# Four of the next tile's projection groups moved into the output projection's loop, and a shorter rounding sequence on VectorE

## The chip, the cores and the metric

One Trainium2 chip, all 8 of its cores, one launch. Each core works on one of the 8 sequences of the batch; no core waits for another, but they share the chip's memory. The metric is the device time in microseconds (us) of the slowest core. Engines: TensorE (PE) multiplies matrices, VectorE (DVE), ScalarE (ACT) and GpSimd (POOL) work elementwise, and DMAs are issued from instruction queues, here above all from the one of SyncE (SP).

## The reference

`x` is 8 sequences of 2048 tokens with 1024 features. The kernel computes

```
xz = x @ Win.T ; xi, z = split(xz)                 # 2 x 2048 features
lam = exp(-8 * softplus(omega) * sigmoid(xi @ Wl.T + bl))
v   = xi @ Wv.T + bv
h_t = lam_t * (h_{t-1} - 2 v_t (v_t.h_{t-1}) / (v_t.v_t)) + (1 - lam_t) * xi_t
x1  = layernorm(x + (silu(z) * h) @ Wout.T)
xq  = clip(round(x1 / scale), -127, 127) * scale    # scale: one number
out = layernorm(x1 + xq @ (ternary - 1).T + bias)
```

The change touches the order of work around `Wout` and the `round` in `xq`.

## The kernel before

A core takes its 2048 tokens in 8 tiles of 256 tokens. Every operation is recorded in program order by `Rec.do` into one list for each engine; an engine executes its own list strictly in that order, and waits on semaphores only where the recorded tokens (`waits=`) say so. DMAs recorded for "sync" stand in SP's list, so a waiting DMA holds up every DMA behind it.

The stages of a tile, in PE's order:

- **lambda and v projections** (L290 to L360, L466 to L538): bf16 matmuls, the weights (`WLV`) streamed in 1 MB steps.
- **gram, chain 0, dhg 0, chain 1, dhg 1**: the recurrence, solved in two chunks of 128 tokens. `chain` alternates small PE and ACT steps; `dhg` runs on VectorE and GpSimd and ends in `LAMb`, the bf16 high and low parts of silu(z)*h.
- **output projection** (L836 to L896): for both halves `dg` of the 1024 output features and 16 slices `ic`, 2 x 3 bf16 matmuls of 128x512. In tile 0 the weights come as f32, 256 KB for each `ic` (`w_out`), VectorE splits them (L853, L858) and two stores write the parts to `wos`; SP's order is load, two stores (which wait for the split), next load. In the other tiles two slices (a *pair*) are loaded at once from `wos`, 2 x 256 KB, into one of two buffers; a load waits until the matmuls of the pair two earlier are done (`wou_free`).
- **layer norm, rounding, transposes, FFN**, for each chunk `tc` of 128 tokens: VectorE adds the residual (L941), `ln` normalises, then eight VectorE instructions on 128x1024 f32 round (L947 to L965). PE transposes the result (L972) as soon as the last of them, L965, is done, and multiplies with the ternary weights (`WFF`). VectorE goes to chunk 1 only after chunk 0's L965.

Into these stages the *first* projection of the **next** tile (`x @ Win.T`) is woven, in 32 *groups* (`emit_s1_group`): a 512 KB load of weights on SP into one of two `WIN` slots (free when the group two earlier is done), eight f32 matmuls (16 records in the trace) into bank `ec % 3`, and an eviction. Groups 0 to 15 give `xi`, 16 to 31 `z`. `pump(n)` emits up to n groups at that place in all lists: 7 ahead of chain 0, one for each of its 7 steps, 2 in chain 1, then 8 at L823 (groups 16 to 23), 2 and 1 before the two chunks' transposes, and 5 at the tile's end. A z group's eviction (L266) overwrites `ZS`, so it waits for `zgate`, the end of dhg 1. With three banks, PE can run groups 16, 17 and 18 while dhg 1 works; group 19 waits for L266. In the last tile there is no next tile, and `pump` does nothing.

Of the kernel before, what the change touches and what calls it, by code (L numbers as in the profile page):

```python
# [8 lines left out]
AL = mybir.AluOpType  # L9
# [36 lines left out]
def build(n_tiles=8):  # L46
    T = n_tiles * TT
    nc = bass.Bass("TRN2", target_bir_lowering=False)
    r = Rec()
# [82 lines left out]
    FFS = sb("FFS", [128, D], F32)  # L132
# [39 lines left out]
    for k in range(NDC):  # L172
# [3 lines left out]
                  waits=(t_cv,))  # L176
        t_cv = r.do("vector", lambda e, a=stg[:, sl * 1024:(sl + 1) * 1024],
                    o=WFF[:, k * D:(k + 1) * D]:
                    e.tensor_scalar_add(o, a, -1.0),
                    waits=(t_l,), inc="dv")  # L180
    t_wffn = t_cv
    t1 = r.do("scalar", lambda e: e.activation(WOM2[:, :], WOM[:, :], AF.Exp),
              waits=(t_pro,), inc="ac")
    t1 = r.do("scalar", lambda e: e.activation(WOM2[:, :], WOM2[:, :], AF.Ln, bias=1.0),
              waits=(t1,), inc="ac")
    t_wom = r.do("vector", lambda e: e.tensor_scalar_mul(WOM2[:, :], WOM2[:, :], -8.0),
                 waits=(t1,), inc="dv")
    t_wom = r.do("vector", lambda e: e.tensor_scalar_mul(WOMN[:, :], WOM2[:, :], -1.0),
                 waits=(t_wom,), inc="dv")
    t_zro = r.do("vector", lambda e: e.memset(ZRO[:, :], 0.0), inc="dv")  # L190
    t_s1 = r.do("vector", lambda e: e.tensor_scalar_max(A1[0:1, 0:1], A1[0:1, 0:1], 1e-5),
                waits=(t_sc,), inc="dv")
    t_s2 = mm(pb[4][:, 0:1], CON[0:1, 0:128], A1[0:1, 0:1], True, True,
              waits=(t_s1, t_con), inc="pe")
    t_s3 = r.do("vector", lambda e: e.tensor_copy(SB_[:, :], pb[4][:, 0:1]),
                waits=(t_s2,), inc="dv")
    drain[4] = t_s3
    t_rs = r.do("vector", lambda e: e.reciprocal(RSC[:, :], SB_[:, :]),
                waits=(t_s3,), inc="dv")
# [74 lines left out]
    for tile in range(n_tiles):  # L274
# [9 lines left out]
        for tc in range(TT // 128):  # L284
            t_xtm = dma("gpsimd", XTM[:, xto + tc * D:xto + (tc + 1) * D],
                        d_xtm[t0 + tc * 128:t0 + (tc + 1) * 128, :], "dxt",
                        waits=(xtm_free[0],))
        t_lam = [None] * NIC
        t_sig = [None] * NIC
        for jc in range(NIC):  # L290
            sl = jc % 2
            if tile == 0:
# [4 lines left out]
                else:  # L297
# [3 lines left out]
                          waits=(tjsp[p],))  # L301
# [3 lines left out]
                            waits=(t_l, tjmm2[p], tjout2[p], tjsp[p]),  # L305
                            inc=jsem)
# [3 lines left out]
                               waits=(t_js,), inc=jsem)  # L310
                dma("sync", d_wls[jc][:, 0:N], wslotb[:, 0:N], "dgl%d" % p,
                    waits=(tjsp[p],))
# [4 lines left out]
            else:  # L317
# [3 lines left out]
                          waits=(wlv_free[sl],) + split_done["wl"])  # L321
                t_w2 = dma("sync", wslotb[:, N:2 * N], d_wls[jc][:, N:2 * N],
                           "dl%d" % (sl + 2),
                           waits=(wlv_free[sl],) + split_done["wl"])
# [11 lines left out]
            for ic in range(NIC):  # L336
# [3 lines left out]
                   waits=(t_xi[NIC - 1],) if ic == 0 else ())  # L340
            for ic in range(NIC):
# [4 lines left out]
                         waits=(t_w2,) if ic == 0 else (),  # L346
                         inc="pe" if ic == NIC - 1 else None)
# [4 lines left out]
            if jc % 2 == 1:  # L352
                for j2 in (jc - 1, jc):
                    tev = r.do("scalar", lambda e, o=fm(KK, j2, 0, TT),
                               i=pb[bank][:, (j2 % 2) * TT:(j2 % 2) * TT + TT],
                               b=BLc[:, j2:j2 + 1]:
                               e.activation(o, i, AF.Sigmoid, bias=b),  # L357
                               waits=(tok,) + tuple(t_hprev), inc="ac")
# [3 lines left out]
        for jc in range(NIC):  # L362
            t_lam[jc] = r.do("scalar", lambda e, o=fm(LAM, jc, 0, TT),
                             i=fm(KK, jc, 0, TT), s=WOM2[:, jc:jc + 1]:
                             e.activation(o, i, AF.Exp, scale=s),  # L365
                             waits=(t_wom, t_sig[jc], t_gprev), inc="ac")
        for jc in range(NIC):
# [3 lines left out]
                              waits=(t_lam[jc],), inc="ac")  # L371
# [43 lines left out]
        if tile != 0:  # L415
            t_rb = r.do("vector", lambda e: e.reduce_sum(
                SB0[:, :].unsqueeze(2), fm3(LAM, 0, L), X),
                waits=(t_bh, t_state_pe), inc="dv")
            t_rb = r.do("vector", lambda e: e.tensor_add(
                SB0[:, :], SB0[:, :], STATE[:, :]),  # L420
                waits=(t_rb, t_state), inc="dv")
# [44 lines left out]
        for jc in range(NIC):  # L466
            sl = jc % 2
            if tile == 0:
# [4 lines left out]
                else:  # L473
# [3 lines left out]
                          waits=(tjsp[p],))  # L477
# [3 lines left out]
                            waits=(t_l, tjmm2[p], tjout2[p], tjsp[p]),  # L481
                            inc=jsem)
# [3 lines left out]
                               waits=(t_js,), inc=jsem)  # L486
                dma("sync", d_wvs[jc][:, 0:N], wslotb[:, 0:N], "dgv%d" % p,
                    waits=(tjsp[p],))
# [4 lines left out]
            else:  # L493
# [3 lines left out]
                          waits=(wlv_free[sl],) + split_done["wv"])  # L497
                t_w2 = dma("sync", wslotb[:, N:2 * N], d_wvs[jc][:, N:2 * N],
                           "dl%d" % (sl + 2),
                           waits=(wlv_free[sl],) + split_done["wv"])  # L500
# [11 lines left out]
            for ic in range(NIC):  # L512
# [3 lines left out]
                   waits=(t_xi[NIC - 1],) if ic == 0 else ())  # L516
# [34 lines left out]
        if tile == 0:  # L551
# [7 lines left out]
            for ic in range(NIC):  # L559
# [8 lines left out]
                       waits=(tok,), inc="dv")  # L568
# [32 lines left out]
        def pump(n=1):  # L601
            for _ in range(n):
                if s1n is None or s1n["ec"] >= 2 * NIC:
                    return
                if s1n["ec"] >= NIC and s1n["zgate"] is None:
                    return
                emit_s1_group(s1n)
# [212 lines left out]
        t_gfull = t_g21  # L820
        if s1n is not None:
            s1n["zgate"] = list(t_g21)
        pump(8)  # L823
        t_state = r.do("vector", lambda e, i=fm3(GC, TT - 1, TT).squeeze(2):
                       e.tensor_copy(STATE[:, :], i),
                       waits=(t_state_pe,) + tuple(t_h), inc="dv")
# [9 lines left out]
        for dg in range(2):  # L836
            for ic in range(NIC):
                sl = (ic // 2) % 2
                if tile == 0:
                    p = ic % 2  # L840
                    if p == 0:
                        slotf = WOU[:, 0:512]
                        wslotb = WOU.bitcast(BF16)[:, 2048:3072]
                    else:
                        slotf = Y1[:, 0:512]
                        wslotb = Y1.bitcast(BF16)[:, 2048:3072]
                    jeng, jsem = "vector", "dv"
                    kw = (tjout2[1], tjsp[1]) if wofirst[1] and p == 1 else ()
                    wofirst[p] = False
                    t_l = dma("sync", slotf, d_wo[dg, ic], "wo%d" % p,  # L850
                              waits=(wosp[p],) + kw)
                    t_js = r.do(jeng, lambda e, o=wslotb[:, 0:512], i=slotf:
                                e.tensor_copy(o, i),  # L853
                                waits=(t_l, womm[p], woout[p], wosp[p]) + kw,
                                inc=jsem)
                    wosp[p] = r.do(jeng, lambda e, o=wslotb[:, 512:1024],
                                   i=slotf, h=wslotb[:, 0:512]:
                                   e.tensor_tensor(o, i, h, AL.subtract),  # L858
                                   waits=(t_js,), inc=jsem)
                    dma("sync",  # L860
                        d_wos[dg, ic // 2][:, (ic % 2) * 1024:(ic % 2) * 1024 + 512],
                        wslotb[:, 0:512], "dgo%d" % p, waits=(wosp[p],))
                    woout[p] = dma("sync",
                                   d_wos[dg, ic // 2][:, (ic % 2) * 1024 + 512:
                                                      (ic % 2) * 1024 + 1024],
                                   wslotb[:, 512:1024], "dgo%d" % p, waits=())
                    t_w = wosp[p]
                    split_done["wo"] = (woout[0], woout[1], wosp[0], wosp[1])
                else:
                    slotb = WOU.bitcast(BF16)[:, sl * 2048:(sl + 1) * 2048]  # L870
                    if ic % 2 == 0:
                        t_wo2 = dma("sync", slotb[:, 0:1024],
                                    d_wos[dg, ic // 2][:, 0:1024],
                                    "wo%d" % sl,
                                    waits=(wou_free[sl],) + split_done["wo"])
                        t_wo2b = dma("sync", slotb[:, 1024:2048],
                                     d_wos[dg, ic // 2][:, 1024:2048],
                                     "wo%d" % (sl + 2), waits=())
                    t_w = t_wo2 if ic % 2 == 0 else t_wo2b
                    wslotb = slotb[:, (ic % 2) * 1024:(ic % 2 + 1) * 1024]  # L880
                for tc in range(TT // 128):
                    bank = 4 + 2 * dg + tc
                    gh = LAMb[:, ic * 2 * TT + tc * 256: ic * 2 * TT + tc * 256 + 128]
                    gl = LAMb[:, ic * 2 * TT + tc * 256 + 128:
                              ic * 2 * TT + tc * 256 + 256]
                    w0 = ((t_w, drain.get(bank)) + tuple(t_g2c[tc])) \
                        if ic == 0 else (t_w,)
                    mm(pb[bank][:, 0:512], gh, wslotb[:, 0:512],
                       ic == 0, False, waits=w0)
                    mm(pb[bank][:, 0:512], gl, wslotb[:, 0:512], False, False)  # L890
                    gtok[2 * dg + tc] = mm(pb[bank][:, 0:512], gh,
                                           wslotb[:, 512:1024],
                                           False, ic == NIC - 1, inc="pe")
                wou_free[sl] = gtok[2 * dg + (TT // 128) - 1]
                t_jmm = wou_free[sl]
                womm[ic % 2] = t_jmm  # L896

        if tile == 0:
            split_done["stage"] = split_done["stage"] + (wosp[1], woout[1])
# [29 lines left out]
        for tc in range(TT // 128):  # L929
# [3 lines left out]
            for dg in range(2):  # L933
# [13 lines left out]
            tq = r.do("vector", lambda e, o=r1s, i=y1s: e.tensor_scalar(  # L947
                o, i, RSC[:, :], 127.0, AL.mult, AL.min),
                waits=(t_y1[tc], t_rs, txq), inc="dv")
            tq = r.do("vector", lambda e, o=r1s: e.tensor_scalar_max(o, o, -127.0),  # L950
                      waits=(tq,), inc="dv")
            tq = r.do("vector", lambda e, o=FFSI[:, :], i=r1s: e.tensor_copy(o, i),
                      waits=(tq,) + split_done["stage"], inc="dv")
            tq = r.do("vector", lambda e, o=scr, i=FFSI[:, :]: e.tensor_copy(o, i),
                      waits=(tq,), inc="dv")
            tq = r.do("vector", lambda e, o=FFS[:, :], i=r1s, k=scr:
                      e.scalar_tensor_tensor(o, i, -0.5, k, AL.add, AL.is_ge),
                      waits=(tq,), inc="dv")
            tq = r.do("vector", lambda e, o=r1s, k=scr:
                      e.scalar_tensor_tensor(o, o, 0.5, k, AL.add, AL.is_le),  # L960
                      waits=(tq,), inc="dv")
            tq = r.do("vector", lambda e, o=FFS[:, :], i=r1s:
                      e.tensor_sub(o, o, i), waits=(tq,), inc="dv")
            txq = r.do("vector", lambda e, o=r1s, i=FFS[:, :], k=scr:
                       e.tensor_add(o, i, k), waits=(tq,), inc="dv")  # L965
            txq_l[tc] = txq
            pump(2 if tc == 0 else 1)
            for k8 in range(NDC):
# [132 lines left out]
```

How the kernel before makes its waits and increments, by code:

```python
            def body(e):  # L1035
                for fn, waits, inc, by in r.ops[eng]:
                    for s, v in waits:
                        e.wait_ge(sems[s], v)
                    ins = fn(e)
                    if inc is not None:
                        ins.then_inc(sems[inc], by)
```

## Time and profile before

| | us |
|---|---|
| median of 2 runs (lowest, highest) | 4176.14 (4088.86, 4263.42) |
| the profiled execution, own time | 4078.83 |
| its span on the slowest core (all cores: 4049.1 to 4077.2) | 4077.2 |
| TensorE matmul busy in it | 3268.0 (80%) |
| VectorE, ScalarE, GpSimd busy | 1306.8 (32%), 564.1 (14%), 220.2 (5%) |
| mean granted TensorE clock, share of full speed | 0.896 |
| chain that ended last: PE, DMA, DVE, issue, ACT | 56%, 21%, 10%, 6%, 4% |

PE is busy four fifths of the span and everything else less than a third, so what counts is the time in which PE waits, and the time in which it runs at the lower of its two clock levels (1.2 instead of 2.4 GHz; a granted clock of 0.50 and 1.00 in the rows). A timeline row gives start, duration, engine, line, operation, how many, and in brackets how long the engine was idle before it and what ended that.

### The profile page before, as it was taken

What the parts mean: (1) busy time and instruction counts of PE and PEld (TensorE: products, weight loads), DVE (VectorE), ACT (ScalarE), POOL (GpSimd) and SP (SyncE); (2) the same over time, 40 slices, a digit from 0 to 9 for tenths busy, and PEclk for the clock granted to TensorE, in tenths of its full rate; (3) what the DMA queues carried; (4) which work ended last, traced back from release to release, by engine and by line L of the source; (5) the groups of instructions that cost most, each with busy time, mean ns of one, the idle gap of its engine ahead of it and who ended that gap; (6) DMA issues with size and microseconds to landing.
All of it is one profiled execution on the core that took longest, in us unless ns stands there. A gap on an engine that the chain in (4) does not pass through costs nothing.

```text
span 4077.2 us, 53180 instructions; the slowest of 8 cores (4049.1 to 4077.2 us)
## 1 busy us (share of the span) xinstructions
PE 3268.0 (80%) x20717; PEld 2553.6 (63%) x20764; DVE 1306.8 (32%) x2380; ACT 564.1 (14%) x1454; POOL 220.2 (5%) x164
## 2 busy tenths in 40 slices
PE   4856668647997799878997799788987799879965
PEld 3644456315886488746886489656875488647852
DVE  1023553223243305223333306222423305321553
ACT  0001001002201112102201111101201120111211
POOL 0000001100002000010002000110002000100020
PEclk9977779758998899988998899998998899999967
DMA  4455532234632355234632364244622464245602
GB/s 141 144 157 176 172 127 83 86 102 134 202 117 80 119 197 186 78 114 151 206 105 83 123 208 156 83 131 159 199 95 95 140 191 131 88 129 165 197 21 83
DMA packets 171369, 545.28 MB, mean 134 GB/s; under 512 B 20083, under 2 KB 28660, under 8 KB 167028
## 3 DMA queue, kind: packets, MB, share of 16 engines
q1 hardware_dynamic: 163444, 516.72, 39.7%
q0 software_dynamic: 5376, 16.78, 1.3%
q10 hardware_dynamic: 2304, 8.39, 0.5%
q8 instruction: 169, 2.77, 0.3%
q14 instruction: 76, 0.62, 0.1%
HBM read 491.48 MB, written 50.33 MB: 133 GB/s over the span
## 4 chain that ended last, share of the span: by engine, by line
PE 56%; DMA 21%; DVE 10%; issue 6%; ACT 4%; POOL 2%; SPq 1%; DVEq 0%; ACTq 0%; POOLq 0%
PE pb L152 54%; DMA WIN<-w_in 5%; DMA WOU<-wos 4%; DMA WLV<-wvs 2%; DMA WLV<-w_l 2%; DMA WLV<-wls 2%; DMA R<-w_l 2%; DMA WLV<-w_v 1%; DVE XFM L765 1%; SPq L157 1%; DMA Y<-w_out 1%; DMA WOU<-w_out 1%; DMA R<-w_v 1%; DMA WIN<-w_ffn 1%; PE pb L709 1%
## 5 line engine op out<-in xcount | busy, mean ns | idle before, releaser
L152 PE MATMUL pb<-XI,WLV 128*128 128x256 bf16 x11520 | 1301.3, 276 | 103.0 <-DVE WLV L309 44.4
L152 PEld LDWEIGHTS pb<-XI,WLV 128*128 128x128 bf16 x11520 | 1137.9, 99 | 266.3 <-issue 118.8
L152 PE MATMUL pb<-XFM,WIN 128*128 128x256 f32 x4096 | 1003.9, 404 | 116.5 <-DMA WIN<-w_in 61.3
L152 PEld LDWEIGHTS pb<-XFM,WIN 128*128 128x128 f32 x4096 | 815.4, 203 | 277.8 <-issue 158.1
L152 PE MATMUL pb<-WOU,LAM 128*128 128x512 bf16 x1409 | 340.5, 393 | 97.4 <-DVE WOU L858 40.3
L388 DVE TENSOR_TENSOR_SCAN GC<-LAM,ZRO 128x256 f32<-128x256 f32 x128 | 88.6, 692 | 754.5 <-ACT LAM L365 742.0
L152 PEld LDWEIGHTS pb<-WOU,LAM 128*128 128x128 bf16 x1440 | 136.8, 99 | 300.8 <-issue 163.5
L260 DVE TENSOR_TENSOR XI<-pb,XI 128x256 bf16<-128x256 f32 x128 | 53.6, 423 | 498.9 <-ACT XI L257 487.9
L757 POOL TENSOR_TENSOR KK<-VB,GB 128x512 f32<-128x512 f32 x16 | 44.5, 2778 | 2656.1 <-ACT GB L733 2656.1
L152 PE MATMUL pb<-XI,Y 128*128 128x256 bf16 x768 | 118.4, 331 | 80.1 <-DVE Y L309 41.3
L941 DVE TENSOR_TENSOR R<-pb,XTM 128x512 f32<-128x512 f32 x32 | 22.1, 690 | 480.3 <-PE pb L152 476.7
L152 PEld LDWEIGHTS pb<-XI,Y 128*128 128x128 bf16 x768 | 89.5, 118 | 108.9 <-issue 84.1
L152 PE MATMUL pb<-VB,KSC 128*128 128x128 f32 x768 | 140.7, 291 | 4.4 <-DVE KSC L432 4.4
L357 ACT ACTIVATE KK<-pb,BLc 128x256 f32<-128x256 f32 x128 | 53.7, 471 | 646.8 <-PE pb L152 646.7
L535 ACT ACTIVATE VB<-pb,BVc 128x256 f32<-128x256 f32 x128 | 53.6, 469 | 632.6 <-PE pb L152 632.6
L972 PE MATMUL pb<-IDE,R 128*128 128x128 f32 x128 | 41.2, 423 | 105.3 <-DVE R L965 90.1
L257 ACT ACTIVATE XI<-pb 128x256 bf16<-128x256 f32 x128 | 49.2, 384 | 491.2 <-PE pb L152 487.1
L152 PEld LDWEIGHTS pb<-VB,KSC 128*128 128x128 f32 x768 | 108.2, 194 | 4.5 <-issue 4.4
L765 DVE TENSOR_TENSOR_SCAN XFM<-LAM,STATE,KK 128x128 f32<-128x128 f32 x256 | 110.0, 502 | 2.6 <-DVE KK L757 1.8
L152 PE MATMUL pb<-LAM,KSC 128*128 128x128 f32 x512 | 110.5, 298 | 0.0
L392 DVE TENSOR_TENSOR_SCAN KK<-KK,ZRO 128x256 f32<-128x256 f32 x128 | 88.6, 692 | 53.1 <-ACT KK L370 40.3
L972 PEld LDWEIGHTS pb<-IDE,R 128*128 128x128 f32 x128 | 21.7, 184 | 126.8 <-issue 125.3
(167 smaller groups left out, 2234.3 us busy)
## 6 DMA issues: line engine op xcount, KB each, us to landing
WIN<-w_in SPq DMA_DIRECT2D x256, 512.0 KB, 3.6
WLV<-wls SPq DMA_DIRECT2D x224, 512.0 KB, 5.0
WLV<-wvs SPq DMA_DIRECT2D x224, 512.0 KB, 4.9
WOU<-wos SPq DMA_DIRECT2D x224, 256.0 KB, 3.2
XFM<-x_fm POOLq DMA_DIRECT2D x64, 128.0 KB, 8.5
XTM<-x_tm POOLq DMA_DIRECT2D x16, 512.0 KB, 5.0
WLV<-w_l SPq DMA_DIRECT2D x8, 1024.0 KB, 7.8
wls<-WLV SPq DMA_DIRECT2D x16, 512.0 KB, 4.9
```

What stands on the lines that cost most here:

```text
L152: return e.matmul(o, l, rr, start=st, stop=sp)
L157: return e.dma_start(d, s)
L257: e.activation(o, i, AF.Copy), waits=(tok,), inc="ac")
L260: e.tensor_tensor(o, i, h, AL.subtract),
L357: e.activation(o, i, AF.Sigmoid, bias=b),
L388: e.tensor_tensor_scan(o, d0, ZRO[:, 0:TT], 1.0, AL.mult, AL.add),
L392: e.tensor_tensor_scan(o, o, ZRO[:, 0:TT], 1.0, AL.mult, AL.add),
L535: e.activation(o, i, AF.Identity, bias=b),
L709: t_tp = r.do("tensor", lambda e, i=nxt_p: e.transpose(pb[7][:, 0:128], i[:, :], IDE[:, :]), waits=(t_ep, drain.get(7)), inc="pe")
L757: e.tensor_mul(o, i0, i1),
L765: e.tensor_tensor_scan(o, d0, d1, i0, AL.add, AL.subtract),
L972: e.transpose(o, i, IDE[:, :]),
```

## The change

Two edits. (1) `pump(8)` after dhg 1 becomes `pump(4)`; the other four groups (20 to 23) are emitted inside the output projection, one after every fourth slice of its first half (`dg == 0`, `ic` = 3, 7, 11, 15). (2) The rounding adds 0.5 in the clip instruction, converts to int and back, compares once and subtracts: six VectorE instructions instead of eight.

```diff
         if s1n is not None:
             s1n["zgate"] = list(t_g21)
-        pump(8)
+        pump(4)
@@ output projection, end of the ic loop
                 womm[ic % 2] = t_jmm
+                if ic % 4 == 3 and dg == 0:
+                    pump(1)
@@ rounding, for each tc
-            tq = r.do("vector", lambda e, o=r1s: e.tensor_scalar_max(o, o, -127.0),
-                      waits=(tq,), inc="dv")
+            tq = r.do("vector", lambda e, o=r1s: e.tensor_scalar(
+                o, o, -127.0, 0.5, AL.max, AL.add), waits=(tq,), inc="dv")
             tq = r.do("vector", lambda e, o=FFSI[:, :], i=r1s: e.tensor_copy(o, i),
                       waits=(tq,) + split_done["stage"], inc="dv")
             tq = r.do("vector", lambda e, o=scr, i=FFSI[:, :]: e.tensor_copy(o, i),
                       waits=(tq,), inc="dv")
-            tq = r.do("vector", lambda e, o=FFS[:, :], i=r1s, k=scr:
-                      e.scalar_tensor_tensor(o, i, -0.5, k, AL.add, AL.is_ge),
+            tq = r.do("vector", lambda e, o=FFS[:, :], i0=scr, i1=r1s:
+                      e.tensor_tensor(o, i0, i1, AL.is_gt),
                       waits=(tq,), inc="dv")
-            tq = r.do("vector", lambda e, o=r1s, k=scr:
-                      e.scalar_tensor_tensor(o, o, 0.5, k, AL.add, AL.is_le),
-                      waits=(tq,), inc="dv")
-            tq = r.do("vector", lambda e, o=FFS[:, :], i=r1s:
-                      e.tensor_sub(o, o, i), waits=(tq,), inc="dv")
-            txq = r.do("vector", lambda e, o=r1s, i=FFS[:, :], k=scr:
-                       e.tensor_add(o, i, k), waits=(tq,), inc="dv")
+            txq = r.do("vector", lambda e, o=r1s, i0=scr, i1=FFS[:, :]:
+                       e.tensor_sub(o, i0, i1), waits=(tq,), inc="dv")
```

## Rows read from the trace of the kernel before

**Rows 1.** Waits of TensorE, whole span: who waited for whom, us, times, longest
```profile
PE pb L972 <- DVE R L965: 90.1, 16, 14.5
PE pb L152 <- DMA WIN<-w_in: 61.3, 65, 5.2
PE pb L152 <- DVE Y L858: 46.3, 16, 4.7
PE pb L152 <- DVE WOU L858: 40.3, 15, 3.6
PE pb L152 <- DMA WOU<-wos: 36.0, 57, 1.9
```
**Rows 2.** VectorE by line: operation, count | busy, mean ns | idle before
```profile
L963 DVE TENSOR_TENSOR FFS<-FFS,R 128x1024 f32<-128x1024 f32 x16 | 19.6, 1225 | 1.7
L957 DVE SCALAR_TENSOR_TENSOR FFS<-R,XFM 128x1024 f32<-128x1024 f32 x16 | 19.6, 1225 | 1.7
...
L950 DVE TENSOR_SCALAR R<-R 128x1024 f32<-128x1024 f32 x16 | 11.1, 694 | 2.1 <-DVE R L947 0.5
```
**Rows 3.** Timeline, tile 1, rounding and transposes of both chunks
```profile
1391.78 1.23 DVE L960 SCALAR_TENSOR_TENSOR R<-R,XFM 128x1024 f32<-128x1024 f32 x1
1393.11 1.23 DVE L963 TENSOR_TENSOR FFS<-FFS,R 128x1024 f32<-128x1024 f32 x1
...
1395.92 0.66 PE L972 MATMUL pb<-IDE,R 128*128 128x128 f32 x2 [7.36 <-DVE R L965]
...
1413.00 0.66 PE L972 MATMUL pb<-IDE,R 128*128 128x128 f32 x2 [3.52 <-DVE R L965]
```
**Rows 4.** Timeline, the shortest such waits: tile 0 chunk 0, tile 4 chunk 1
```profile
943.00 0.41 PE L972 MATMUL pb<-IDE,R 128*128 128x128 f32 x2 [4.21 <-DVE R L965]
...
2774.43 0.66 PE L972 MATMUL pb<-IDE,R 128*128 128x128 f32 x2 [3.27 <-DVE R L965]
```
**Rows 5.** Windows, groups 19 to 23, tiles 1 to 6: us, PE busy, PEclk, DMA share, GB/s
```profile
1310.80:1332.97 22.17, 20.87 (x80) 0.88 0.38 119
...
sum 132.98, PE 124.96; mean PE 20.83
```
**Rows 6.** Windows, output projection's first half (dg 0), tiles 1 to 6, summed
```profile
sum 138.54, PE 125.32; mean PE 20.89
```
**Rows 7.** Windows, output projection's second half (dg 1), tiles 1 to 6, summed
```profile
sum 151.93, PE 129.53; mean PE 21.59
```
**Rows 8.** Timeline, tile 1: two groups, then slices 0 to 3 and 4, 5 of dg 0
```profile
1381.50 7.07 PE L152 MATMUL pb<-XFM,WIN 128*128 128x256 f32 x32
...
1332.97 5.13 PE L152 MATMUL pb<-WOU,LAM 128*128 128x512 bf16 x23
1338.69 2.75 PE L152 MATMUL pb<-WOU,LAM 128*128 128x512 bf16 x12 [0.59 <-DMA WOU<-wos]
```
**Rows 9.** DMA issues, page: operation, count, KB each, median us to landing
```profile
WIN<-w_in SPq DMA_DIRECT2D x256, 512.0 KB, 3.6
```
**Rows 10.** Timeline, tile 0, start of the output projection
```profile
738.51 1.12 DVE L825 COPY STATE<-GC 128x16 f32<-128x16 f32 x1
...
755.95 0.43 SPq L157 DMA_DIRECT2D WOU<-w_out  x1
...
760.06 0.43 DVE L853 CAST WOU<-WOU 128x512 bf16<-128x512 f32 x1 [20.43 <-DMA WOU<-w_out]
760.59 0.69 DVE L858 TENSOR_TENSOR WOU<-WOU 128x512 bf16<-128x512 f32 x1
...
762.25 0.40 SPq L157 DMA_DIRECT2D Y<-w_out  x1
...
765.19 0.43 DVE L853 CAST Y<-Y 128x512 bf16<-128x512 f32 x1 [3.90 <-DMA Y<-w_out]
```
**Rows 11.** Windows, all engines' busy, then PEclk, DMA share, GB/s
```profile
1417.00:1422.70 5.70, 5.41 (x14) 2.10 (x16) 2.27 (x7) 2.45 (x4) 0.00 (x0) 0.56 0.10 39
1434.00:1450.00 16.00, 10.14 (x33) 8.10 (x34) 0.00 (x0) 0.77 (x2) 4.03 (x8) 0.79 0.89 306
```

## The prediction, on record before the changed kernel ran

> **What bounds the kernel now.** I read the page first (its figures stand in the table above): TensorE is busy 80% of the span and no other engine more than 32%, so a change pays only where it shortens a wait of TensorE, or lets it run at its upper clock level. The second view is therefore the list of TensorE's waits over the span [rows 1]. The longest is the one of the transposes (L972) for the last rounding instruction on VectorE (L965): 90.1 us in 16 waits, one for each chunk of each tile. Then come the loads of the first projection's weights (WIN, 61.3 us), the splits of tile 0's output weights on VectorE (46.3 + 40.3 us), and the pair loads of the other tiles (36.0 us in 57). The change aims at all four. The third view is the timeline around each place, and the fourth the windows that add up the same stretch of tiles 1 to 6, to see how much time a stretch takes beyond its matmuls.
>
> **Rounding: minus 42.6 us.** Two of eight instructions go. A tensor-with-tensor instruction on 128x1024 f32 takes 1225 ns, with a compare (L957) or without (L963) [rows 2]; the new compare and subtract cost that much each, and the clip takes a second constant. No row has such a clip with two constants at work; L950 takes 694 ns with one [rows 2], and I take the same, since in L957 two operations cost no more than one in L963. What goes is so two instructions of the 1225 ns kind, and in the timeline one starts 1.33 us after the other (1391.78, 1393.11) [rows 3]: 2.66 us for a chunk.
>
> It lies on the path. PE waits 7.36 us for chunk 0 and 3.52 us for chunk 1 of tile 1 [rows 3]; the shortest of the 16 waits are 4.21 for a chunk 0 and 3.27 for a chunk 1 [rows 4]. Chunk 0's transposes so start 2.66 us sooner in every tile. Chunk 1's VectorE work begins when chunk 0's ends, so its end comes 5.32 us sooner, while PE, which has one group and the FFN between, arrives 2.66 us sooner; of the wait of 3.27 us 0.61 is left, and no wait runs out. The one place where VectorE waits for another engine on this way is the square on ScalarE, queued behind the copies of chunk 0's transposes, which come sooner by the same 2.66 us. What follows (FFN, output, next tile) hangs on PE's and VectorE's own progress and moves along. 8 tiles x 5.32 = 42.6 us. Next to be late is VectorE again, by 0.6 to 1.5 us for chunk 1.
>
> **Moved groups, tiles 1 to 6: minus 29 us.** The matmuls themselves are neither fewer nor faster, and no result is due earlier: layer norm needs both halves of the output projection, and these come after all eight groups in either order. What can be gained is time waiting for loads. At the upper clock level a group takes 7.07 / 2 = 3.54 us, and four slices of the output projection (24 matmuls, 23 of them recorded) 5.13 us, so one half of 16 slices takes 20.5 us [rows 8]. Against that:
>
> Groups 19 to 23 take 132.98 us in six tiles, and 6 x 5 x 3.54 = 106.2 of it is work. Their window has a granted clock of 0.88, hence 0.24 of 22.17 us at the lower level of 1.2 GHz, which costs 2.66 us, six times 16.0 [rows 5]. 10.8 us are waits for WIN loads. The first half takes 138.54, of which 123.1 is work: 15.4 us of waits [rows 6]. The second takes 151.93: 28.8 us of waits, in 8 pairs each tile [rows 7].
>
> After the change SP reaches the first two pairs' loads right behind group 19's, and group 20's right behind these, all while dhg 1 still runs. PE then has pair, pair, group, pair, pair, group. A pair's load starts when the pair two earlier is done, and until it is needed PE has another pair (2.56 us) and a group (3.54): 6.1 us instead of 2.56. In the old order a pair came late by 0.59 us [rows 8], so I estimate its load at some 3.2 us. A group's load, issued behind the pair of two places before, has at least 8.6 us against a median of 3.6 [rows 9]. The bytes fit: two pairs and a group are 1.57 MB in 8.66 us, 182 GB/s, and in a window of the same tile the DMAs moved 306 GB/s [rows 11]. So I take 13 of the 15.4 us, 9 of the 10.8, and two eighths of the second half's 28.8 (its first two pairs now load under the last group and the pair beside it), 7.2: together 29. The bounds are 33.4, all of it, and 8, if the loads that are bunched two pairs and a group together land late. The evictions of the moved groups run on ScalarE, which has nothing else there, and use banks 0 to 2, while the output projection uses 4 to 7. The wait for dhg 1 ahead of group 19 stays, and so does the lower clock behind it.
>
> **Tile 0: minus 12 us.** Here the output projection is a chain on SP: load, split, stores, next load, and PE only follows. The chain's first load is issued at 755.95, because four groups' WIN loads stand ahead of it, and its split ends at 760.59 + 0.69 = 761.28 [rows 10]. After the change that load stands behind group 19's, issued while dhg 1 runs, and the split is free to start once VectorE has done L825, at 739.63; it ends at 739.63 + 1.22 = 740.9. The chain starts 20.4 us sooner. Against it, four WIN loads now stand inside it. What one costs there no row shows. From below: the load at 755.95 had a WIN load ahead of it and was split 4.11 us after its issue, the next one, with two stores ahead, 2.94 us after [rows 10], so 1.2, and with one more issue of 0.43 on SP 1.6 us. From above: 524 KB at the 306 GB/s of rows 11 take 1.7 us, and at half that rate 3.4; with the issue 3.9. I take 2.1, nearer to the row of the same queue: 4 x 2.1 = 8.4, leaving 12 us; the bounds are 14 and 5. The matmuls of the four groups hide in PE's 86.6 us of waiting for the splits [rows 1]; at 1.2 GHz they take 4 x 7.1 = 28.
>
> The Trainium skill, page "DMA: Bandwidth & Descriptors", section "Queues, rings and completion order", says that the DMAs of one issuing engine are consumed in ring order, so the whole of a WIN load would have to be fetched before the load behind it. By that each of the four costs a full transfer, and the gain of tile 0 lies at the lower bound; the two landings of rows 10 say that part of it overlaps.
>
> **Sum.** 42.6 + 29 + 12 = 83.6 us off the profiled execution's own 4078.83: 3995 us, 2.05% less. Of the two runs shown one was disturbed (4263.42) and the median is the mean of both; the other, 4088.86, lies 0.2% above the profiled one, and it is these two that the forecast is for.
>
> **Rivals.**
> *The clock stays up in the FFN (0.18).* Behind the transposes the FFN now starts at 1.2 GHz: from 1417.00 to 1422.70 the granted clock is 0.56 [rows 11], after a wait of 3.52 us [rows 3] and the transposes. With 0.9 us of wait left, the clock may not fall between group and FFN. The window's work at 2.4 GHz would take 5.70 x 0.56 = 3.2 us, 2.5 less; in chunk 1 of seven tiles and chunk 0 of tile 0 (4.21 us of wait becomes 1.55) that is 20 us: 3975. Against it: the transposes are still there. The Trainium skill, page "TensorE: Matmul & The Clock Gate", section "HAM oscillation — how this bites in real kernels", has it that idle gaps between bursts of matmuls make each burst start cold; by that rule closing the gaps pays twice. The trace agrees that the clock is low behind these gaps, and no row shows a short one.
>
> *The loads only move (0.18).* If pairs and groups that are issued together land late together, the waits leave the first half and come back, and tiles 1 to 6 give nothing: 4078.8 - 42.6 - 12 = 4024. For it: the second half waits 4.8 us a tile with the pairs alone [rows 7]. Against: the slack of 6.1 us.
>
> *SP holds the groups' loads back (0.03), slower.* A moved group's load stands in SP's list behind the loads of two pairs that wait for PE. Were it issued only when PE is there, PE would wait its 3.6 us [rows 9] and then run the group at 1.2 GHz, 3.5 us more: 7.1 us for each of 28 groups, 199 us, and 4078.8 - 42.6 + 199 = 4235. It turns the sign from 1.5 us a group on. Against: each stands behind waits for the pair two earlier, not the last.
>
> *The rounding does not get shorter at its end (0.03)*: if a compare into f32 ran at twice 1225 ns, half the gain goes: 4016. L957 speaks against it.
>
> **How the numbers follow.** The forecast has 0.58, and its own range from the bounds above is 3989 (29 becomes 33.4, and 12 becomes 14) to 4023 (8 and 5). The range for 8 in 10 takes in the clock rival below, 3989 - 20 = 3969, and the moved loads above, at tile 0's lower bound 4078.8 - 42.6 - 5 = 4031; only the slower case lies outside. Changes under 2% are about what a measurement of this kernel can't tell from none; 2% is 3997. Of the forecast's 0.58 a little over half lies below that: with the clock's 0.18 this makes 0.52 for faster by over 2%; 0.45 within; 0.03 slower.
>
> **What would show it.** The 16 waits for rounding fall from 90.1 to 90.1 - 16 x 2.66 = 47.5 us; VectorE loses 32 x 1.225 = 39 us of busy time. In tiles 1 to 6 the stretch from group 19 to the end of the first half takes 132.98 + 138.54 - 22 = 249.5 us in sum, with pair waits only in the second half, whose sum falls from 151.93 to about 145. In tile 0 the first weight load is issued before L825 ends, and the time from L825 to the end of the output projection falls by 12 us. It would be wrong if chunk 1's wait stays at 3 us or more, if waits for WIN appear in the first half, or if TensorE's mean clock falls below 0.896.

## The result, and the profile after

The changed kernel takes 3987.72 us (median of 11 runs), its profiled execution 3985.67 us against 4078.83. The ratio to the kernel before is **0.9758, 95% interval 0.9743 to 0.9773**: 2.4% less. In some executions the cores of one die, or of both, ran with a lower clock and took longer; the ratios leave these out, and the plain median of before (4182.34 of 10 runs) does not.

TensorE's waits, whole span, slowest core of the changed kernel (L962 and L969 are now the rounding's last instruction and the transposes), beside [rows 1]:

```profile
PE pb L152 <- DMA WIN<-w_in: 72.7, 67, 7.9
...
PE pb L969 <- DVE R L962: 40.3, 9, 11.5
...
PE pb L152 <- DVE WOU L858: 35.8, 11, 3.9
PE pb L152 <- DVE Y L858: 33.5, 14, 3.8
...
PE pb L152 <- DMA WOU<-wos: 17.7, 32, 2.3
...
PE pb L969 <- ACT ZS L266: 7.6, 4, 1.9
...
PE pb L969 <- DVE R L1003: 5.7, 3, 1.9
```

The transposes wait 40.3 + 7.6 + 5.7 = 53.6 us instead of 90.1 (47.5 were forecast), and in 7 of 16 places what ends last is no longer the rounding. In three of these the list names L1003, a VectorE instruction that ends at about that time; in the timeline the transposes start 0.14 us behind the end of the group's eviction (L266) in all seven. Waits for pair loads are halved (36.0 to 17.7), waits for tile 0's splits fall from 86.6 to 69.3. Waits for WIN do not fall: 72.7 on this core, 60.5 on core 6, the core of [rows 1], where they were 61.3, and 64.6 against 56.4 in the mean of the eight cores. The 5.8 us of them between group 19 and the projection's end in tiles 1 to 6 are gone; but 10.9 us (1.0 before) now stand in tile 0's projection, where PE waits for the chain of splits in any case.

VectorE's new compare, and the clip with two constants, mean ns as in [rows 2]:

```profile
L959 DVE TENSOR_TENSOR FFS<-XFM,R 128x1024 f32<-128x1024 f32 x16 | 19.6, 1226 | 1.7
...
L952 DVE TENSOR_SCALAR R<-R 128x1024 f32<-128x1024 f32 x16 | 11.1, 694 | 1.7
```

The compare costs what a subtraction does (1226 ns) and the second constant nothing (694 ns), as taken.

Tile 1, rounding and transposes of both chunks, the counterpart of [rows 3]:

```profile
1359.16 1.22 DVE L962 TENSOR_TENSOR R<-XFM,FFS 128x1024 f32<-128x1024 f32 x1
1360.64 0.41 PE L969 MATMUL pb<-IDE,R 128*128 128x128 f32 x2 [2.60 <-DVE R L962]
...
1370.11 3.62 PE L152 MATMUL pb<-XFM,WIN 128*128 128x256 f32 x16
...
1373.30 1.23 DVE L962 TENSOR_TENSOR R<-XFM,FFS 128x1024 f32<-128x1024 f32 x1
1373.80 1.28 ACT L266 ACT_TABLE_LOAD   x1 [6.37 <-PE pb L152]
1375.10 0.38 ACT L266 ACTIVATE ZS<-pb 128x256 f32<-128x256 f32 x1
1375.62 0.41 PE L969 MATMUL pb<-IDE,R 128*128 128x128 f32 x2 [1.90 <-ACT ZS L266]
```

For chunk 1 the rounding ends at 1374.53, but the first transpose goes into bank 2, which the group just ahead has filled, and ScalarE first loads a table (1.28 us) and then evicts it: 1375.48. That is a wait which stood behind the one that was shortened.

The output projection of tile 1:

```profile
1284.53 6.62 PE L152 MATMUL pb<-XFM,WIN 128*128 128x256 f32 x16 [8.41 <-ACT ZS L266]
1290.98 5.34 PE L152 MATMUL pb<-WOU,LAM 128*128 128x512 bf16 x24
1296.16 3.62 PE L152 MATMUL pb<-XFM,WIN 128*128 128x256 f32 x16
1299.62 5.91 PE L152 MATMUL pb<-WOU,LAM 128*128 128x512 bf16 x24
...
1331.94 5.34 PE L152 MATMUL pb<-WOU,LAM 128*128 128x512 bf16 x24 [0.21 <-DMA WOU<-wos]
```

Behind group 19, which still waits for dhg 1, there is no bracket up to the end of the first half: no wait is left in it, for a pair or for a group. The first pair wait is in the second half. It is the same in all of tiles 1 to 6 on all eight cores, where before this stretch had 6.5 to 15.6 us of pair waits and 2.7 to 9.4 of waits for WIN. The windows from group 19 to the end of the second half, tiles 1 to 6 (us, PE busy, PEclk, DMA share, GB/s):

```profile
1284.53:1348.58 64.05, 62.96 (x271) 0.94 0.47 150
...
sum 390.71, PE 375.46; mean PE 62.58
```

Before, the same stretch is [rows 5] to [rows 7] together: 132.98 + 138.54 + 151.93 = 423.45 us. The clock is not the reason: one minus the granted clock, added up over this stretch, is 16.5 us before and 17.3 after (means over the six cores that have all matmul records). TensorE's idle time falls from 38.5 to 12.5 us; the other 8 us are time of the matmuls themselves, and no run shows why.

Tile 0, the start of its projection, against [rows 10], and the first group inside it:

```profile
721.67 0.42 SPq L157 DMA_DIRECT2D WOU<-w_out  x1
...
729.16 1.12 DVE L825 COPY STATE<-GC 128x16 f32<-128x16 f32 x1
...
730.72 0.69 DVE L858 TENSOR_TENSOR WOU<-WOU 128x512 bf16<-128x512 f32 x1
...
749.23 0.39 SPq L157 DMA_DIRECT2D WIN<-w_in  x1
749.66 0.45 SPq L157 DMA_DIRECT2D WOU<-w_out  x1
...
754.07 0.43 DVE L853 CAST WOU<-WOU 128x512 bf16<-128x512 f32 x1 [5.81 <-DMA WOU<-w_out]
```

The chain's first load is issued 7.5 us ahead of L825 instead of 17.4 after it, and its split ends 1.1 us after L825. With a group's load ahead, VectorE waits 5.81 us for the next weights, instead of about 4.0 in the cycles without.

**Where the time went**, means over the eight cores of both profiled executions, read from their timelines (the projection ends with its last matmul): all in all 96.8 us less. From the projection's end to chunk 1's transposes 40.6 less; chunk 1's transposes themselves 2.9, and the FFN behind them 2.9; tile 0 from L825 to the projection's end 13.4; tiles 1 to 6 from group 19 to the projection's end 33.3; the remaining stages, which nothing was done to, 3.7.

### The profile page after: what moved, and what is told of

The parts are those of the page before. It is cut to its first block, busy times and chain, and to the rows that moved or that the text cites. A ratio compares the mean times of both kernels' runs of the same rounds, so it can differ in the third digit from the quotient of the medians.

```text
span 3984.1 us, 53145 instructions; the slowest of 8 cores (3945.0 to 3984.1 us)
## 1 busy us (share of the span) xinstructions
PE 3254.0 (82%) x20764; PEld 2555.8 (64%) x20764; DVE 1266.6 (32%) x2348; ACT 562.8 (14%) x1454; POOL 219.9 (6%) x164
## 4 chain that ended last, share of the span: by engine, by line
PE 60%; DMA 19%; DVE 9%; issue 5%; ACT 4%; POOL 1%; SPq 1%; DVEq 0%; ACTq 0%; POOLq 0%
PE pb L152 58%; DMA WIN<-w_in 5%; DMA WOU<-wos 2%; DMA WLV<-wls 2%; DMA WLV<-wvs 2%; DMA WLV<-w_l 2%; DMA R<-w_v 1%; DVE XFM L765 1%; DMA R<-w_l 1%; DMA WLV<-w_v 1%; SPq L157 1%; DMA Y<-w_out 1%; DMA WOU<-w_out 1%; DMA WIN<-w_ffn 1%; PE pb L709 1%
## 5 line engine op out<-in xcount | busy, mean ns | idle before, releaser
L152 PE MATMUL pb<-XFM,WIN 128*128 128x256 f32 x4096 | 1009.1, 405 | 126.7 <-DMA WIN<-w_in 72.7
L266 ACT ACTIVATE ZS<-pb 128x256 f32<-128x256 f32 x128 | 46.8, 384 | 503.1 <-PE pb L152 502.8
L152 PE MATMUL pb<-WFF,XNT 128*128 128x512 bf16 x256 | 88.5, 522 | 8.3 <-ACT XNT L973 8.3
```

The costliest lines, as they stand in the source:

```text
L152: return e.matmul(o, l, rr, start=st, stop=sp)
L266: e.activation(o, i, AF.Silu),
```

## The experiments

The theory: each edit removes its own wait, the rounding at the transposes and the moved groups at the loads, and they add up. The rivals are those on record before, and "it is enough to move the groups away from the projection's front".

**Each edit alone.** `e1_rounding` and `f1_rounding` are one kernel: the change without `pump(4)` and the pumps in the loop. `e2_groups` and `f2_groups` are the kernel before with only these:

```diff
-        pump(8)
+        pump(4)
...
+                if ic % 4 == 3 and dg == 0:
+                    pump(1)
```

> Only the shorter rounding; the eight groups stand ahead of the output projection as before. Theory (each edit removes its own wait, and the two add up): the wait of chunk 0's transposes for VectorE shortens by 2.66 us and chunk 1's place by 5.32 us in each of 8 tiles, 41 to 43 us in all, so a ratio to the kernel before of 0.990 (0.989 to 0.991), with the output projection's two halves unchanged. Rival (the shorter rounding only pays where the moved groups leave room, or is eaten by the next wait in line): less than 20 us, a ratio above 0.995.

> The shorter rounding alone, timed once more, since the first timing found too few undisturbed executions for a ratio. Theory (the edits add up): 41 to 43 us in the stretches from the output projection's end to chunk 1's transposes, a ratio of 0.990 to the kernel before. Rival (it needs the moved groups): above 0.995.

> Only the moved groups; the rounding has its eight instructions. Theory (waits for loads go): 12 us in tile 0 and 29 to 34 in tiles 1 to 6, 41 to 47 us in all and a ratio of 0.989 (0.988 to 0.990); pair waits on the output weights fall from 36 us to about 18. Rival (the loads only move, and the second half pays for the first): only tile 0's 12 us, a ratio of 0.997. If the two edits add up, the savings of this kernel and of the one with the rounding alone make the 2.4% of the whole change.

> The moved groups alone, timed once more for the same reason. Theory: 45 us, a ratio of 0.989, so that with the rounding alone the two make the 0.976 of both; the stretch from L825 to the output projection's end gives 12 to 13 us in tile 0 and 5 to 6 in each of tiles 1 to 6. Rival (the loads only move): 0.997.

`e1_rounding` has no ratio. In its profile, on cores 4 to 7, the stretch from the projection's end to chunk 1's transposes is 39.9 us shorter than on the same cores before, and the one from group 19 to the projection's end in tiles 1 to 6 is 3.7 shorter. `f1_rounding`: 0.9891 (0.9832 to 0.9951), the first of these stretches 38.1 us shorter.

The moved groups alone: 0.9923 (0.9821 to 1.0025), which tells nothing, and in `f2_groups` 0.9898 (0.9858 to 0.9937), which excludes the rival's 0.997. Its stretches came out below what was expected, 11.8 us less in tile 0 and 26.3 in tiles 1 to 6, 4.4 a tile; but on cores 4 and 5 a lowered clock cost 42 us of the latter (one minus the granted clock, added up), where it cost 16 to 18 before. Against `f1_rounding` on the same chip, where the groups stand as before, they are 14.0 and 39.0 us shorter.

The product of the two second ratios is 0.979; that of the whole change, 0.976, lies within what the intervals allow. The waits say more than these ratios. Rounding alone (`f1_rounding`; the transposes are L967):

```profile
PE pb L967 <- DVE R L960: 41.3, 9, 11.5
PE pb L152 <- DMA WOU<-wos: 29.8, 45, 2.4
...
PE pb L967 <- ACT ZS L266: 12.0, 7, 1.9
```

and the groups alone (`f2_groups`; L974):

```profile
PE pb L974 <- DVE R L967: 91.2, 16, 14.5
...
PE pb L152 <- DMA WOU<-wos: 16.8, 27, 2.1
```

Each edit leaves the other's wait where it was: with the groups alone the 16 waits for the rounding are still 91.2 us (90.1 before), and with the rounding alone the pair waits are 29.8 us on core 5, where they were 30.6. With the rounding alone the eviction of the group is already the last to end in 7 places, so that wait does not come from the moved groups. The rival that one edit needs the other falls by these stretches and waits; the ratio of `f1_rounding` alone, with an interval up to 0.9951, would not quite do.

**Tile 0 alone** (`pump(4 if tile == 0 else 8)`, and `tile == 0 and` in the loop's condition).

> The groups moved in tile 0 alone, rounding as before. Theory: the chain of load, split and store starts 20.4 us sooner and pays 2.1 us for each of four loads standing in it: 12 us, a ratio of 0.997, and a time from L825 to the end of the projection of tile 0 that is 12 to 13 us shorter; no other tile changes. Rival (a whole transfer is paid for each load in the chain): 5 us or less, 0.999.

0.994 (0.9882 to 0.9998). The interval is too wide for 12 us; the stretch is not. From L825 to the transposes, core 3:

```profile
730.20:926.24 196.04, 103.08 (x305) 0.70 0.35 106
```

The same stretch before, on core 6, is 204.49 us (738.51 to 943.00). Over cores 2 to 5 of both executions it is 13.9 us shorter, so by this a group's load in the chain costs (20.4 - 13.9) / 4 = 1.6 us. Read directly, from one split to the next, a cycle with a group's load takes 7.3 us and one without 5.3 (means over eight cores, 32 and 216 cycles), 2.0 us more; in the changed kernel it is 7.2 and 5.4, 1.8 more. That is a little under the 2.1 taken, and the rival, which leaves 5 us or less, falls.

**The banks of the transposes.**

```diff
-                bank = 2 + k8 % 2
+                bank = 4 + tc + 2 * (k8 % 2)
```

> The changed kernel, with the transposes' results in the two banks that the FFN of the same chunk uses afterwards, instead of banks 2 and 3. In the changed kernel chunk 1's transposes wait for ScalarE's eviction of the group ahead of them, which lies in bank 2, or for VectorE. Theory: that wait (7.6 us in four places, the rest hidden) goes from the list and chunk 1 waits for VectorE alone, 0.3 to 1.5 us a tile; the time falls by 2 to 5 us, which one run can't tell. Rival (the rounding's end is what counts, the eviction only comes last by a little): the list changes and the time does not.

On core 3:

```profile
PE pb L969 <- DVE R L962: 48.5, 16, 11.5
PE pb L969 <- ACT XNT L973: 17.4, 48, 0.8
```

All 16 waits are for the rounding again. From the end of the rounding to the start of chunk 1's transposes it is 0.15 us in every tile, 1.2 us in sum; in the changed kernel it is 0.5 to 1.0 us in tiles 0 to 6, 5.5 in sum (means of eight cores). So the eviction did cost, 4.4 us in all. The kernel was timed once, 4056.18 us, and one time can't show 2 to 5 us.

**The groups in one place**, between the halves:

```diff
-                if ic % 4 == 3 and dg == 0:
-                    pump(1)
+                if ic == NIC - 1 and dg == 0:
+                    pump(4)
```

> The changed kernel, but with its four moved groups all in one place, between the output projection's halves, instead of one after every fourth slice. Theory (it is the time a group gives to the loads of the pairs behind it that pays): the first half's waits come back, 2.6 us in each of tiles 1 to 6, with some 0.5 to 1 for the groups' own loads; in tile 0 the loads of the second half stand behind the last group's load, which waits for the second group, 10 to 14 us. 26 to 36 us above the changed kernel, a ratio of 0.983 to the kernel before. Rival (it is enough that the groups no longer stand ahead of the projection): 0.976 as the changed kernel.

0.9868 (0.9818 to 0.9918): of the 2.4% only 1.3 are left, about what the rounding gives alone, and the interval excludes the rival's 0.976. In tile 0 SP shows the reason foretold, on core 3:

```profile
817.00 11.53 SPq L157 DMA_DIRECT2D WIN<-w_in  x4
828.58 0.43 SPq L157 DMA_DIRECT2D WOU<-w_out  x1
```

The next load of the chain is issued 11.6 us after the first of the groups' loads, of which the last waits for PE. In tiles 1 to 6, the waits for pairs are back, 29.9 us on this core against 17.7:

```profile
PE pb L152 <- DMA WOU<-wos: 29.9, 49, 2.0
```

Against the changed kernel tile 0's projection is 9.9 us longer and the stretch of tiles 1 to 6 37.0 (means of eight cores), 47 us where 26 to 36 were expected. A part of it is a lowered clock on some cores; on core 4, where the clock costs about the same (17 and 16 us), the stretch takes 424.8 us, against 387.0 in the changed kernel and 422.3 before. In one lump the four groups so give nothing in tiles 1 to 6: it is the time which a group gives to the loads behind it that pays, not the move.

**More of it.** `e7_both_halves` drops `and dg == 0`, so that eight groups stand in the projection and one is left at the tile's end. `e8_both_three` also has the banks above and `pump(3 if tc == 0 else 1)`; `g2_both_three` is the same kernel, timed again beside the changed kernel, `g1_changed`.

> The changed kernel, with a group after every fourth slice of both halves of the output projection, eight instead of four; four fewer are left for the tile's end. Theory (a group between two pairs gives each pair's load 3.5 us more, and hides its wait): the second half's waits, about 3.4 us a tile, go too, 17 us in tiles 1 to 6, and at the tile's end four groups that wait there for loads beside the next tile's activations are gone, 10 to 28 us more: 3950 us, a ratio of 0.967 to the kernel before. Rival (the bytes are the bound there and the waits come back at the next stage's weights): 17 us at most, 0.972. Rival (loads only move): 0.976 as without it.

> As the one before, and with three groups instead of two ahead of chunk 0's transposes, whose results go to the two banks of that chunk's FFN so that they don't wait for a group's eviction. Theory (chunk 0's transposes wait for VectorE some 4.6 us after two groups, so a third one of 3.54 us is free there, and is one less at the tile's end): 7 x 3.54 = 25 us and some 5 us for the banks, about 3920 us, a ratio of 0.959. Rival (the tile's end hides one group more or less behind its loads): no faster than the one before by more than 5 us.

> The changed kernel itself, timed on the same chip as the next one, to compare the two and to see whether its gain holds on another chip. Theory: a ratio of 0.976 to the kernel before (0.973 to 0.979). Rival (part of the 2.4% was that one chip's): above 0.980.

> The kernel with a group after every fourth slice of both halves, three groups ahead of chunk 0's transposes and these in the FFN's banks, beside the changed kernel. Theory: 22 to 32 us faster than the changed kernel, a ratio to the kernel before of 0.967 to 0.970, since its per-core spans were 32 us shorter in the mean. Rival (the waits for the next stage's weights take it all back): the same ratio as the changed kernel's.

In this order to the kernel before, without `g1_changed`: 0.9688 (0.9642 to 0.9733), 0.9664 (0.9595 to 0.9733) and 0.9623 (0.9575 to 0.9671). `e7_both_halves` agrees with its forecast of 0.967 and excludes 0.976, but not the rival's 0.972; `e8_both_three` misses its 0.959, and whether it beats `e7_both_halves` by more than 5 us these intervals can't tell. `g1_changed` has no ratio: two of its executions, 4007.35 and 4047.44 us, can be set beside six of before on that chip, from 4097.79 to 4124.28 with a median of 4105.1. They are 0.976 and 0.986 of it, so whether the 2.4% hold on another chip is left open. `g2_both_three`, with 3952.18 and 3953.66 us beside them, is faster than the changed kernel, by more than the 22 to 32 us expected, on two executions each. The waits of `e8_both_three`, core 3:

```profile
PE pb L152 <- DMA WIN<-w_in: 40.5, 41, 3.2
...
PE pb L152 <- DMA WLV<-wls: 33.5, 30, 3.9
PE pb L969 <- DVE R L962: 32.7, 9, 11.5
...
PE pb L152 <- DMA WOU<-wos: 2.9, 5, 1.7
```

The pair waits are all but gone, and of WIN's a good part. The first rival of `e7_both_halves` is half right: with fewer groups at the tile's end the next stage's weights come late, 33.5 us for `wls` where the changed kernel waits 6.2, so a part of the gain is lost again there.

**The clock of the FFN.** `e9_no_round` takes the wait away, by leaving out the four instructions after the clip.

> The changed kernel with the rounding left out: after the clip the four instructions (to int, back, compare, subtract) are gone, so the output lacks the rounding; all else is as it was. Some 4.1 us less VectorE work for each chunk. Theory (the FFN's lower clock comes from the transposes ahead of it, not from the wait alone): chunk 0's transposes start 4 us sooner, chunk 1's wait for the group's eviction, 35 to 50 us in all, and the FFN's 16 matmuls take 5 us as before. Rival (with no wait between group and transposes the clock stays at 2.4 GHz): the FFN takes 3.5 us, 1.6 less in 14 places or 22 us more, 60 to 70 us in all.

0.9707 (0.9628 to 0.9785), too wide to tell 35 from 70 us. From the projection's end to chunk 1's transposes it is 38.4 us shorter than the changed kernel (mean of eight cores), of which chunk 0's FFN gives 6.8; that is the theory's 35 to 50 and not the rival's 60 to 70. The windows show the clock: chunk 0's FFN in tiles 0, 2 and 1 of `e9_no_round`, core 3 (us, busy of PE, PEld, DVE, ACT and POOL, PEclk):

```profile
935.43:938.88 3.45, 3.45 (x16) 1.66 (x17) 0.57 (x4) 2.38 (x4) 0.00 (x0) 1.00 0.02 5
1822.79:1826.24 3.45, 3.45 (x16) 1.65 (x17) 0.56 (x4) 2.38 (x4) 0.00 (x0) 1.00 0.00 0
1383.56:1389.06 5.50, 5.50 (x16) 2.15 (x17) 2.39 (x6) 2.38 (x4) 0.00 (x0) 0.62 0.00 0
```

and chunk 1's transposes and FFN in tile 1 of the changed kernel, against 0.56 for the FFN in [rows 11]:

```profile
1375.60:1379.00 3.40, 1.82 (x8) 1.03 (x8) 3.05 (x4) 1.86 (x9) 0.00 (x0) 1.00 0.35 145
1379.10:1384.20 5.10, 5.10 (x16) 2.06 (x17) 2.08 (x6) 2.35 (x4) 0.00 (x0) 0.67 0.01 5
```

With no wait between group and transposes the FFN can run wholly at 2.4 GHz (3.45 us), but does so in some tiles only. Over tiles 0 to 6 of all eight cores, with at most 0.44 us of wait ahead of the transposes, 35 of chunk 0's 56 FFNs have no time at 1.2 GHz; in the other 21 the clock falls with no wait to account for it. Chunk 1's, with 1.9 us of wait, have some in all 56. In the changed kernel it is 3 of 56 without, behind waits of 3.5 us in the mean, and none of 56 behind 2.0 us; before, none of 112. So both theory and rival are right in part. Chunk 1's transposes in the changed kernel have a granted clock of 0.83 in the mean (1.00 in 9 of 56), where before, behind 4.1 us of wait, it was 0.54.

## Why the prediction was right or wrong

It said 3995 us, 83.6 us off the profiled execution, with a range of 3969 to 4031; the median came out at 3987.72 and the profiled execution at 3985.67, 93 us off, and 96.8 in the mean of the cores. The three terms of the sum, 83.6 us, measured 87.3; 5.8 us of clock, taken as nothing, and 3.7 us elsewhere came on top. What failed is first the footing of the sum, and then the sentence "no wait runs out" in the term of the rounding. By its steps:

- **The step that failed: the footing.** The sum takes 83.6 us off the profiled execution (4078.83) and says of it and of the 4088.86 that "it is these two that the forecast is for". The table's time for the kernel before is the median of its two runs, 4176.14, which lies 97 us higher. At the measured ratio of 0.9758 that median becomes 4176.14 x 0.9758 = 4075 us, 44 above the range's upper end. The range has terms for the loads and for the clock and puts the choice of footing at nothing, although the text names the 4263.42 us that make the gap, and the gap is larger than the effect. On the footing that it chose it holds: 3987.72 lies in the range. The change itself, 2.4% instead of the 2.05% forecast, is somewhat larger, for the reasons that follow.
- **Rounding, 42.6 forecast, 40.6 measured.** The prices are right to the nanosecond, and chunk 0 gets its 2.66 us (21.0 us in eight tiles, mean of the cores). Chunk 1's rounding ends 23.2 us sooner after chunk 0's, where 21.3 were forecast; the surplus of 1.9 us is not explained. The sentence that failed is "no wait runs out" with "next to be late is VectorE again": it looked at VectorE and PE's arrival, and not at the bank that the transpose writes. Group 26 lies in bank 2, and so do the transposes, so its eviction with a table load ends last in 7 of 16 places, and the time from the end of the rounding to chunk 1's transposes grows from 2.0 to 5.5 us: 21.0 + 23.2 - 3.6 = 40.6. The bank experiment takes this wait away. The mistake is small because the eviction ends only about a microsecond behind the rounding, and that the surplus makes up for half of it is luck. The prediction also calls the square the one place where VectorE waits for another engine; it waits for the square root as well (1.68 us in front of L921, tile 1 of the changed kernel).
- **Moved groups in tiles 1 to 6, 29 forecast, 33.3 measured** as the mean of the cores (32.7 between the two slowest): the upper bound, all the waits from group 19 to the end of the first half and a part of the second's. The prediction had withheld 4 us without a row for it. A slip of book-keeping does not touch the sum: group 23 stands behind the first half's last slice, so its 3.5 us count with the second half; the whole stretch was to be 394.5 us and is 390.7.
- **Tile 0, 12 forecast, 13.4 measured.** The chain starts 20.4 us sooner, as worked out. A load inside costs 1.8 to 2.0 us instead of 2.1. The Trainium skill, page "DMA: Bandwidth & Descriptors", section "Queues, rings and completion order", has the descriptors on each DMA engine consumed in ring order, though a later one may finish its write before an earlier one. The trace agrees that the load behind is delayed, by about the 1.7 us that 524 KB take at the 306 GB/s of [rows 11], so it does not speak against that order. What failed is the conclusion that the gain would lie at the lower bound: the 3.9 us a load behind that bound were taken at half that rate.
- **The clock, taken as nothing, a rival of 20 us at 0.18.** It gave 2.9 us in chunk 1's transposes and 2.9 in the FFN behind them (from -1.2 to 6.6 on single cores). The rule of the Trainium skill, page "TensorE: Matmul & The Clock Gate", section "HAM oscillation — how this bites in real kernels", that gaps make each burst start cold, is borne out in part by `e9_no_round`: without a gap 35 of 56 FFNs have no time at 1.2 GHz, with one of 1.9 us none; but in 21 of the 56 the clock falls without a gap. The change leaves 2 to 5 us of wait in nearly all places, so it pays only a little.
- **The rivals that lost.** That the loads only move: pair waits fall from 36.0 to 17.7, with none in the first half. That SP holds the loads back: no wait for WIN from group 19 to the projection's end in tiles 1 to 6. That the compare is dear: 1226 ns.
- **The chances.** 0.45 for less than 2% came from a point that lay 2 us below that line. The 4 us withheld and the 5.8 us of clock put the result beyond it.
- **Open.** 3.7 us lie in stages that the change does not touch; the cores scatter there by more than this from one execution to the next, and no run assigns them.

## What to carry to other kernels

Work that is due later is worth most where it gives time to loads that come late, one piece ahead of each few of them; in one lump the same work gave nothing in tiles 1 to 6 here. When a wait is shortened, ask of the waiting instruction everything that it needs, the bank that it writes included, and not only the operand it was last seen waiting for. And a forecast in microseconds should say on which footing it stands when the runs shown differ by more than the effect.

## What the runs showed of the hardware that was not expected

A table load of 1.28 us in front of a 0.38 us eviction made ScalarE, busy for a seventh of the span, the last to end in front of TensorE. In tile 1 of the changed kernel, behind a wait of 1.90 us, TensorE's clock was granted in full (1.00) in chunk 1's transposes and fell in the FFN (0.67); before, behind 3.52 us, the transposes had 0.50 and the FFN 0.56. With no more than 0.44 us of wait ahead (`e9_no_round`) 35 of 56 FFNs had no time at 1.2 GHz, and 21 had some. And a 512 KB load placed ahead of another in the same queue delayed it by 1.8 to 2.0 us only.
